# Strassen's scheme for the down projection of a fp32 feed-forward, with the work around it cut in halves

## The reference

```
x = act_qdq(x)                       # symmetric 16 bit quantisation, one scale for the whole tensor
up = act_qdq(x @ lpbq_dequant(w_up).T)
gate = act_qdq(x @ lpbq_dequant(w_gate).T)
sig = fixed_qdq_u16(sigmoid(gate))
gate = act_qdq(gate * sig)           # "g2" in the kernel, 1536 x 4096
o = act_qdq(gate * up)               # 1536 x 4096
return o @ lpbq_dequant(w_down).T    # the down projection: 1536 -> 512
```

## Time and profile before

| what | value |
|---|---|
| median of three runs | 4766.68 us |
| the profiled execution: its own time, its span | 4764.43 us, 4762.6 us |
| mean granted TensorE clock | 0.939 |
| TensorE busy over the span | 3990.7 us, 84% |
| VectorE, ScalarE, GpSimd busy | 3482.5 (73%), 2392.1 (50%), 2644.5 us (56%) |
| down projection, first matmul to last | 1698.5 to 2031.8 us |
| HBM traffic | 394 MB read, 228 MB written |

### The profile page before, as it was taken

One profiled execution on the slowest core, in us unless ns is written; L12 is line 12 of the kernel. 1 busy time (PEld: TensorE's weight loads), 2 busy tenths in 40 slices (PEclk: granted clock), 3 DMA queues, 4 the chain that ended last, 5 costly groups with the idle time before them and its releaser, 6 DMA issues. The chain is left out here.

```text
span 4762.6 us, 50359 instructions
## 1 busy us (share of the span) xinstructions
PE 3990.7 (84%) x15892; PEld 2275.5 (48%) x15900; DVE 3482.5 (73%) x3920; ACT 2392.1 (50%) x4711; POOL 2644.5 (56%) x1567
## 2 busy tenths in 40 slices
...
GB/s 111 99 105 76 77 97 182 86 95 102 195 288 275 338 194 210 159 126 180 204 193 85 72 178 62 64 180 59 66 178 64 70 95 243 276 53 18 36 27 36
DMA packets 363928, 625.70 MB, mean 131 GB/s; under 512 B 67238, under 2 KB 152647, under 8 KB 351634
## 3 DMA queue, kind: packets, MB, share of 16 engines
...
HBM read 394.24 MB, written 228.15 MB: 131 GB/s over the span
## 5 line engine op out<-in xcount | busy, mean ns | idle before, releaser
L2534 POOL TENSOR_TENSOR sc_X<-sc_Bm,sc_w 128x1024 f32<-128x1024 f32 x512 | 1191.9, 2362 | 89.4 <-DVE sc_H L2713 63.4
L2556 ACT ACTIVATE sc_A<-sc_dt,keep_A 128x1024 f32<-128x1024 f32 x512 | 581.8, 1137 | 85.2 <-DVE sc_Z L2718 63.6
L2586 ACT ACTIVATE sc_hT<-sc_tp,sc_ct 128x128 f32<-128x128 f32 x2048 | 583.0, 375 | 73.3 <-PE sc_tp L2640 70.3
L2640 PE MATMUL sc_tp<-sc_idn,sc_H 128*128 128x128 f32 x2048 | 316.8, 278 | 221.1 <-issue 142.9
L2661 PE MATMUL sc_yp<-sc_Z,sc_idn 128*128 128x512 f32 x1024 | 490.0, 601 | 9.9 <-ACT sc_yo L2592 9.6
L2640 PEld LDWEIGHTS sc_tp<-sc_idn,sc_H 128*128 128x128 f32 x2048 | 233.6, 141 | 435.5 <-issue 249.5
L2713 DVE TENSOR_TENSOR_SCAN sc_H<-sc_A,sc_X 128x1024 f32<-128x1024 f32 x160 | 359.0, 2275 | 28.2 <-ACT sc_A L2556 15.5
L2713 DVE TENSOR_TENSOR_SCAN sc_H<-sc_A,sc_hc,sc_X 128x1024 f32<-128x1024 f32 x160 | 368.3, 2335 | 2.2 <-ACT sc_A L2556 2.2
L1475 PE MATMUL ff_ps<-ffn_R,hand_w 128*128 128x512 f32 x768 | 330.2, 592 | 1.1 <-ACT ff_o L1588 1.1
L75 POOL TENSOR_TENSOR gp_pbd<-gp_r,ssm_msk 128x512 f32<-128x512 f32 x144 | 182.0, 1264 | 220.3 <-DVE gp_r L478 220.3
L2647 PEld LDWEIGHTS sc_yp<-sc_idn,sc_hT 128*128 128x128 f32 x2048 | 237.8, 141 | 102.5 <-issue 82.8
...
## 6 DMA issues: line engine op xcount, KB each, us to landing
...
```

Of the source, the lines that this page charges most:

```text
L2534: nc.gpsimd.tensor_tensor(X[:, k % RX], Bm[:, n], w[:, j % 2], ALU.mult).then_inc(db, 1)
L2556: nc.scalar.activation(A[:, k % 2], dt[:, j % 2], ACT.Exp, scale=keepA[:, n:n + 1]).then_inc(ex, 1)
L2586: nc.scalar.activation(hT[:, turned(k) % 2, q], tp[:, b * P:(b + 1) * P], ACT.Copy, scale=ct[:, i % 2, q, n:n + 1]).then_inc(tc, 1)
L2640: last = nc.tensor.transpose(tp[:, b * P:(b + 1) * P], H[:, slot(k % NS), h * TB + b * P:h * TB + (b + 1) * P], idn[:])
```

## The change

Blocks 1 to 7 take Strassen's scheme (in the form with 7 products and 15 sums). A block of 512 rows x 1536 hidden x 512 outputs is cut in two along each side. Of the 512 rows, the quarters of 128 with i = 0 form the first half and those with i = 1 the second (`rows_of`); hidden units are split 6 + 6 blocks, outputs 256 + 256. Each of the 7 products is 12 matmuls with 256 columns (`down`).

- Sums over the weights (`down_sums`, 4 of 128 x 1536) are made once by VectorE, into the unused `z`.
- Sums over o (`row_sum`, 4 of 128 x 1536 per block) are made by VectorE and lie over `gd[v]`, whose g2 is no longer needed then. So g2 of block n + 2 can be loaded only when the last product of block n has ended (`dq_`), while up can be loaded after its third (`dr_`).
- The products are not combined with one another: VectorE adds each to the residual rows as it comes (`add_rows(n, q)`, q = 0 to 7, each 128 x 2 x 256). Bank 0 collects three products and is read after each of them, bank 3 collects two; so the product that comes next on a bank waits for the read (`added`).
- Rounding of g2, product and scaling run in halves of 6 hidden blocks. Taking the magic number away from o goes from VectorE to ScalarE (`round_half`), and so does the normalisation (scale `rs`, bias `mrn` = -mean * rs).
- The residual rows have two tiles (`x` and half of `g`).
- VectorE's order is written out anew: the parts of block n + 1's preparation stand between the `add_rows` of block n.

There are 12 more semaphores. The diff, cut to its core:

```diff
+        HD_, HK = D // 2, HB_ // 2
+        rows = xb
+        osum = [[r[:, HB_ * TB + 4 * j * 3 * P:HB_ * TB + 4 * (j + 1) * 3 * P].rearrange("p (k w t) -> p k w t", k=HK, w=2) for j in range(4)] for r in (R1, R0)]
+        dsum = [z.rearrange("p v t -> p (v t)")[:, j * HK * HD_:(j + 1) * HK * HD_].rearrange("p (k c) -> p k c", k=HK) for j in range(4)]
+        dp_, ds_, dr_, dq_, xa, os4, dt4, ng, mrs = [s.sem(n) for n in ("dp", "ds", "dr", "dq", "xa", "os4", "dt4", "ng", "mrs")]
+        rin = [s.sem("rin0"), s.sem("rin1")]
...
-            def load_block(n):
...
+            def load_block_g2(n):
+                for h in range(2):
+                    k = slice(h * HK, (h + 1) * HK)
+                    sp.dma_start(gd[n % 2][:, k], g2_b[:, k, n * TB:(n + 1) * TB]).then_inc(dgi[n % 2][h], 16)
+
+            def load_block_up(n):
+                sp.dma_start(zd[n % 2], up_b[:, :, n * TB:(n + 1) * TB]).then_inc(dzi[n % 2], 16)
+
+            def load_rows(n):
+                sp.dma_start(rows[n % 2], xr[n]).then_inc(rin[n % 2], 16)
...
-                    load_block(0)
...
-
-            for n in range(1, NB):
-                if n == 1:
-                    sp.wait_ge(cmx, 1 + NT_)
-                if n > 1:
-                    sp.wait_ge(dmm, 1 + (n - 1) * NU)
...
+                    load_block_g2(0)
+                    load_block_up(0)
+            load_rows(0)
+            sp.wait_ge(cmx, 1 + NT_)
+            load_block_g2(1)
+            load_block_up(1)
+            load_rows(1)
+            sp.wait_ge(dmm, 1 + NU)
+            load_block_g2(2)
+            load_block_up(2)
+            sp.wait_ge(yok, 1 + NU)
+            load_rows(2)
+            for n in range(3, NB):
+                sp.wait_ge(dr_, 1 + n - 2)
+                sp.wait_ge(os4, 1 + 4 * (n - 2))
+                load_block_up(n)
+                sp.wait_ge(dq_, 1 + 2 * (n - 2))
+                load_block_g2(n)
+                sp.wait_ge(yok, 1 + (n - 1) * NU)
+                load_rows(n)
...
+            def down(n, b, a, m, onto, done):
+                for w in range(2):
+                    for k in range(HK):
+                        last = nc.tensor.matmul(ps[:, n % 2 * NU + b, w * HD_:(w + 1) * HD_], a[:, k, w], m[:, k],
+                                                start=(w == 0 and k == 0 and not onto), stop=(w == 1 and k == HK - 1), skip_group_check=onto)
+                last.then_inc(done, 1)
+
+            def added(n, q):
+
+                pe.wait_ge(xa, 1 + 8 * (n - 1) + q)
+
...
             for n in range(1, NB):
-                v = n % 2
-                pe.wait_ge(r2, 1 + NPC + n)
...
+                pe.wait_ge(r2, 1 + NPC + 2 * n - 1)
+                if n == 2:
+                    pe.wait_ge(res, 1 + NU)
+                if n > 2:
+                    added(n - 2, 8)
+                down(n, 0, rows_of(n, 0, 0), down_of(0, 0), False, dp_)
+                pe.wait_ge(r2, 1 + NPC + 2 * n)
+                down(n, 1, rows_of(n, 0, 1), down_of(1, 0), False, ds_)
+                down(n, 2, rows_of(n, 1, 1), down_sum(3), False, dr_)
+                added(n, 1)
+                down(n, 0, row_sum(n, 1), down_sum(1), True, dp_)
+                down(n, 3, row_sum(n, 0), down_sum(0), False, dq_)
+                added(n, 4)
+                down(n, 0, row_sum(n, 2), down_sum(2), True, dp_)
+                added(n, 5)
+                down(n, 3, row_sum(n, 3), down_of(1, 1), True, dq_)
...
+            def less_magic_half(n, h):
+                v = gd[n % 2][:, h * HK:(h + 1) * HK]
+                act.wait_ge(d1, 1 + half(n, h, 1))
+                nc.scalar.activation(v, v, ACT.Identity, bias=magic[:]).then_inc(d2, 1)
+
+            def round_half(n, h):
+                v = zd[n % 2][:, h * HK:(h + 1) * HK]
+                act.wait_ge(r1, 1 + half(n, h, NPC))
+                nc.scalar.activation(v, v, ACT.Identity, bias=magic[:]).then_inc(r2, 1)
...
             for n in range(NB):
                 if n + 1 < NB:
-                    less_magic_block(n + 1)
+                    for h in range(2):
+                        less_magic_half(n + 1, h)
+                    for h in range(2):
+                        round_half(n + 1, h)
                 nn.take_root(nc, act, n, eps[:])
+                act.wait_ge(mrs, 1 + n + 1)
+                act.wait_ge(yst, 1 + n * 16)
+                for u in range(NU):
+                    nc.scalar.activation(y[:, u], rows[n % 2][:, u], ACT.Identity, scale=nn.rs[:, u:u + 1], bias=mrn[:, u:u + 1]).then_inc(yok, 1)
                 act.wait_ge(yok, 1 + n * NU + NU)
...
+            def round_g2_half(n, h):
+                v = gd[n % 2][:, h * HK:(h + 1) * HK]
+                dve.wait_ge(dgi[n % 2][h], 1 + (n // 2 + 1) * 16)
+                nc.vector.tensor_scalar(v, v, s2.mul, MAGIC, ALU.mult, ALU.add).then_inc(d1, 1)
+
...
+                nc.vector.tensor_tensor(t1, b12, b11, ALU.subtract).then_inc(dt4, 1)
+                nc.vector.tensor_tensor(t3, b22, b12, ALU.subtract).then_inc(dt4, 1)
+                dve.wait_ge(dt4, 1 + 1)
+                nc.vector.tensor_tensor(t2, b22, t1, ALU.subtract).then_inc(dt4, 1)
+                dve.wait_ge(dt4, 1 + 3)
+                nc.vector.tensor_tensor(t4, t2, b21, ALU.subtract).then_inc(dt4, 1)
...
+                s1, s2_, s3, s4 = osum[n % 2]
+                l, r, op, own = ((a21, a22, ALU.add, 0), (s1, a11, ALU.subtract, 1), (a11, a21, ALU.subtract, 0), (a12, s2_, ALU.subtract, 2))[j]
+                dve.wait_ge(r2, 1 + half(n, 1, NPC))
+                dve.wait_ge(os4, 1 + 4 * (n - 1) + own)
+                nc.vector.tensor_tensor(osum[n % 2][j], l, r, op).then_inc(os4, 1)
+
+            def product_part(n, p, parts):
+                k = slice(p * HB_ // parts, (p + 1) * HB_ // parts)
+                o_, gq = zd[n % 2][:, k], gd[n % 2][:, k]
+                dve.wait_ge(d2, 1 + (half(n, p, 1) if n else 1))
                 dve.wait_ge(d3, 1 + n + 1)
                 nc.vector.scalar_tensor_tensor(out=o_, in0=o_, scalar=MAGIC, in1=gq, op0=ALU.subtract, op1=ALU.mult).then_inc(dpr, 1)
...
+            def scale_o(n, h):
+                v = zd[n % 2][:, h * HK:(h + 1) * HK]
+                dve.wait_ge(dpr, 1 + half(n, h, NPC))
+                nc.vector.tensor_scalar(v, v, os_.mul, MAGIC, ALU.mult, ALU.add).then_inc(r1, 1)
...
+            def norm(n):
+                dve.wait_ge(yok, 1 + n * NU)
+                nn.mean_rstd(nc, dve, n)
+                nc.vector.scalar_tensor_tensor(out=mrn[:], in0=nn.mv[:, :, 0], scalar=-1.0, in1=nn.rs[:], op0=ALU.mult, op1=ALU.mult).then_inc(mrs, 1)
...
+
+                i, j, b, scale, sem, count = (
+                    (0, 0, 0, os_.s, dp_, 3 * n - 2), (0, 0, 1, os_.s, ds_, n), (1, 0, 2, nos[:], dr_, n), (0, 1, 0, os_.s, dp_, 3 * n - 1),
+                    (1, 1, 3, os_.s, dq_, 2 * n - 1), (1, 0, 0, os_.s, dp_, 3 * n), (1, 1, 0, os_.s, dp_, 3 * n), (0, 1, 3, os_.s, dq_, 2 * n))[q]
+                v = rows[n % 2].rearrange("p (w i) (j c) -> p w i j c", i=2, j=2)[:, :, i, j]
+                dve.wait_ge(sem, 1 + count)
+                dve.wait_ge(xa, 1 + 8 * (n - 1) + (0, 1, 0, 0, 0, 3, 5, 4)[q])
+                nc.vector.scalar_tensor_tensor(out=v, in0=ps[:, n % 2 * NU + b].rearrange("p (w c) -> p w c", w=2), scalar=scale, in1=v,
+                                               op0=ALU.mult, op1=ALU.add).then_inc(xa, 1)
...
             def finish(n):
-                v = n % 2
-                dve.wait_ge(rin, 1 + n * 16 + 16)
+                add_rows(n, 7)
...
-                    nn.apply(nc, y[:, u], x[:, u], u).then_inc(yok, 1)
+                    dve.wait_ge(xa, 1 + 8 * n)
+                    nc.vector.bn_stats(nn.st[:, u, 0], rows[n % 2][:, u]).then_inc(nn.stats, 1)
+                norm(n)
...
-            for n in range(NB):
-                if n + 1 < NB:
-                    round_g2_block(n + 1)
-                    product(n + 1)
-                    round_o(n + 1)
-                finish(n)
...
+            nc.vector.tensor_scalar(nos[:], os_.s, -1.0, None, ALU.mult).then_inc(ng, 1)
+            dve.wait_ge(ng, 2)
+            down_sums()
+            for h in range(2):
+                round_g2_half(1, h)
+            for h in range(2):
+                product_part(1, h, 2)
+            for h in range(2):
+                scale_o(1, h)
+            for j in range(4):
+                row_sum(1, j)
+            finish_first()
+            for n in range(1, NB):
+                more = n + 1 < NB
+                if n > 1:
+                    finish(n - 1)
+                if more:
+                    round_g2_half(n + 1, 0)
+                dve.wait_ge(rin[n % 2], 1 + (n // 2 + 1) * 16)
+                add_rows(n, 0)
+                if more:
+                    round_g2_half(n + 1, 1)
+                    product_part(n + 1, 0, 2)
+                add_rows(n, 1)
+                if more:
+                    product_part(n + 1, 1, 2)
```

(62 more changed lines are left out.)

54 lines of the change are left out of this document (29 added, 25 removed).

## The result

The changed kernel took 4787.88 us, the median of five runs (4785.10 to 4794.79); the kernel before, 4764.41 us in the runs beside them. The ratio is 1.0047 (95% interval 1.0036 to 1.0058): slower by 0.5%. The forecast was 4782.

The account below looks back on a forecast made before the run. TensorE bounds the kernel before; after the change VectorE's queue would, waiting for block 2's up and the port. Terms sum to +13.0, with 4 for the clock +17: 4781.4 profiled, 4782 median, range 4755 to 4798.

Parts of the forecast that it names:

- block 1: TensorE idles about 20 us ahead of block 1's sixth product, waiting for VectorE's additions; block 2 starts +16.8 us.
- blocks 2 to 5 without the clock: TensorE's last product ends 41.7 us into each block, 0.5 us more than before, four times: +2.0.
- cold last products of these: Last products of blocks 2 to 5 start cold after 5.3 us of idle: 4 us, bounds 0 and 4 x 2.6.
- block 6: No up is left to load in block 6, so it takes 38.7 us: -2.5 us.
- block 7: VectorE prepares nothing in block 7, so it takes 36.05 us: -5.1.
- end: Last product to store: addition, statistics and four normalisations on ScalarE take 7.8 us where it was 6.2: +1.6.
- semaphores: Twelve semaphores in the changed kernel: +0.2.
- the clock: TensorE's clock drops after idle, 1.2 GHz after 4.90 us; a cold start costs up to 2.6 us; 4 taken.
- TensorE's part: 84 matmuls of 256 columns replace 48 of 512: a product 5.15 us, a block 36.05 us instead of 41.2.
- the port: VectorE with two SBUF inputs and GpSimd reading SBUF hold each other off; 3.0 us in a block.
- The 13 us to spare: In the kernel before, VectorE's product for block 2 starts with 13 us to spare before that block's matmuls.
- rival C: TensorE stays the bound from block 2 if g2's second half lands 8.3 us after issue, port not hit; 4749; chance 0.10.

Follow-up runs that it names:

- e5: Changed kernel with block 2's g2 loaded early, add_rows 3 ahead of scalings, 4 ahead of row sums, GpSimd waiting for row sums: 4734.19 us, ratio 0.9926.
- e3: Changed kernel with only block 2's g2 load moved, issued once block 0's product has been made: 4775.68 us, ratio 1.0015 to the kernel before.
- e2: Changed kernel with GpSimd waiting, from block 3 on, for the previous block's four row sums before scaling up: 4758.48 us, ratio 0.9979.
- e1: Changed kernel with only VectorE's order changed, add_rows(n, 4) ahead of the next block's first row sums: 4762.49 us, ratio 0.9987.
- e9: Changed kernel with 12 extra unused matmuls of 256 columns ahead of the wait before the last product of blocks 2 to 5: 4775.80 us, ratio 1.0020.
- e8: Kernel before, without Strassen, with ScalarE rounding o in one piece of 6144 numbers and normalising: 4773.40 us, ratio 1.0015.
- e10: Kernel before with rounding and normalisation on ScalarE, the scaling of o and ScalarE's rounding in two pieces of 3072: 4767.79 us, ratio 1.0003.
- e6: Changed kernel with g2 of block n + 2 loaded in two steps, the first half after block n's fifth product: 4781.80 us, ratio 1.0033.

## Why the prediction was right

| term | forecast | measured, from TensorE's rows |
|---|---|---|
| block 1 (before: 41.7) | +16.8 | 57.5: +15.8 |
| blocks 2 to 5 without the clock | +2.0 | +10.6 in all, less the next row: +1.6 |
| cold last products of these | +4 | 6.94 + 7.56 + 7.84 + 7.99 - 4 x 5.34 = +9.0 |
| block 6 | -2.5 | -3.6 |
| block 7 | -5.1 | -4.9 |
| end | +1.6 | +1.3 |
| semaphores; measured is block 1's start | +0.2 | +0.3 |
| sum to the store | +17 | +19.45 |

The +0.3 is no measure of the semaphores: among the profiles block 1 starts between 1742.3 and 1746.6 us. The sum came close in part by luck: the clock took 5.0 us more than forecast, the terms of block 1, blocks 2 to 5, block 6 and the end together 2.8 less. The forecast for the profiled execution was 4781.4 and it took 4785.10; of these 3.7 us 2.45 arise in the stage and 1.2 behind the store. The median lies another 2.8 us higher, which no term explains.

- *TensorE's part.* Right: a product takes 5.2 us at the full clock, and seven of them gave 36.26 us in e5.
- *Block 1.* Right in mechanism, landing and GpSimd's end (forecast 1770.45, measured 1770.4), and in the scaling that waits for the port. e3 shows the load (12.6 us), e2 the port (4.3 us). Here the price of the cold sixth product was not nothing: it ended the block, 0.3 us behind VectorE's chain, which the forecast had as the last.
- *Blocks 2 to 5.* The forecast idle was 5.3 us, the measured one 5.1 to 5.6. The blocks took 43.6 to 44.2 us where the prediction's sign was 41 to 42; the clock makes the difference. The first row sum took 5.7 us, not 4 to 5: the port held it for 4 us instead of 3.0, as ScalarE's halves ended 0.7 us sooner and GpSimd began 0.4 us later than forecast. e2 shows that the port makes it, e1 that it reaches the last product only through VectorE's order.
- *The clock.* The term that was mis-sized. The bounds were 0 and 2.6 us a block, and I took 1. The row for the upper bound (block 0 against block 1, 2.6 us) was the nearest one, since a gap of 4.90 us had given the lower clock in the earlier trace rows, and I should have stood by it. It measured 1.6 to 2.65 us a block. e9 shows the cause, and the granted clocks of 0.67 to 0.78 agree.
- *What was wrong without changing the sum.* The 13 us to spare (e8, e10). Then the argument against rival C, that no loading order makes the second half of g2 land sooner: loaded in two steps it did (e6). C failed in the changed kernel on both of its conditions, as the second half landed 11 us into the block (VectorE rounds it at 1811.20 in block 2) and the port was hit; it came true where both held, in block 6 of e6. Its outcome, TensorE as the bound, was also there to be had by the order and the port: 36.26 us a block and 4734 us in e5, below the 4749 that I gave it, since block 1 gained too.
